# A state-space block with experts on one core: ScalarE's second decay takes over two of VectorE's waits, C rows in four buffers, tanh written into the activation tile

## What is computed

```python
# attention part: INNER = 512 channels d, 16 states n, T = 512 positions t
dt = softplus(xb @ W_dt + b_dt); A = -exp(A_log); B = xb @ W_B; C = xb @ W_C
def step(h, inp):                              # scanned over t
    x_t, dt_t, B_t, C_t = inp
    h = exp(dt_t[:, :, None] * A) * h + (dt_t * x_t)[:, :, None] * B_t[:, None, :]
    return h, einsum('bdn,bn->bd', h, C_t)
y = (y + D_param * xb) * silu(z);  x = x + ga * (h_in + y @ W_out)
# expert part: every expert is computed for every token and weighted (0 for those not picked)
act = silu(x @ gate_e) * (x @ up_e);  out = sum_e weight_e * (act @ down_e)
```

## Time and profile before

| what | value |
|---|---|
| median of 3 runs | 2757.75 us (2750.83 to 2760.53) |
| the profiled execution, its own time | 2752.47 us |
| its span in the trace | 2750.4 us |
| PE, DVE, POOL, ACT busy (share of the span) | 86%, 87%, 81%, 53% |
| DMA engines, mean rate | 217 GB/s |
| granted TensorE clock, mean | 0.942 |

### The profile page before, as it was taken

One profiled execution on the slowest core, in us unless ns is written; L12 is line 12 of the kernel. 1 busy time (PEld: TensorE's weight loads), 2 busy tenths in 40 slices (PEclk: granted clock), 3 DMA queues, 4 the chain that ended last, 5 costly groups with the idle time before them and its releaser, 6 DMA issues.

```text
span 2750.4 us, 28746 instructions
## 1 busy us (share of the span) xinstructions
PE 2365.5 (86%) x9004; PEld 1687.1 (61%) x9004; DVE 2391.1 (87%) x2386; ACT 1455.0 (53%) x2767; POOL 2234.6 (81%) x1563
## 2 busy tenths in 40 slices
PE   3445798999989899998989999898999989898899
PEld 1212566666756666675666667566666656666678
DVE  2679899989999999999999999989999999999922
ACT  3455556555555655555565555556555555654311
POOL 1678888888988888898988888888888889887922
PEclk7677899999999999999999999999999999999999
DMA  4789899999989899998989999898999989898921
GB/s 114 197 197 252 206 244 223 233 236 221 248 212 247 219 245 233 222 246 210 241 219 248 221 213 249 211 235 219 243 228 218 245 206 244 220 248 214 241 59 50
DMA packets 338378, 596.79 MB, mean 217 GB/s; under 512 B 49696, under 2 KB 160288, under 8 KB 338224
## 3 DMA queue, kind: packets, MB, share of 16 engines
q0 software_dynamic: 72960, 243.30, 46.3%
q1 hardware_dynamic: 265264, 351.64, 41.2%
HBM read 349.89 MB, written 10.06 MB: 131 GB/s over the span
## 4 chain that ended last, share of the span: by engine, by line
PE 51%; POOL 15%; DVE 9%; DMA 8%; issue 8%; ACT 7%; SPq 0%; POOLq 0%; DVEq 0%; ACTq 0%
PE wbank L498 16%; PE mbank L510 9%; PE wbank L400 8%; POOL unit L1183 6%; DMA gsum<-unit 6%; DVE hbank L717 5%; PE wbank L440 4%; PE wbank L526 3%; PE wbank L388 3%; POOL act L1150 2%; POOL gsum L1195 2%; PE wbank L411 2%; ACT z L839 2%; PE wbank L523 2%; POOL rstd L1085 2%
## 5 line engine op out<-in xcount | busy, mean ns | idle before, releaser
L1183 POOL TENSOR_TENSOR unit<-dtx,b_bc 128x1024 f32<-128x1024 f32 x512 | 1353.2, 2653 | 4.6 <-DMA gsum<-unit 2.3
L717 DVE TENSOR_TENSOR_SCAN hbank<-hbank,unit 128x1024 f32<-128x1024 f32 x512 | 1173.0, 2291 | 94.7 <-ACT hbank L1012 73.8
L1012 ACT ACTIVATE hbank<-dt,a_neg 128x512 f32<-128x512 f32 x1024 | 667.8, 680 | 266.3 <-DVE unit L731 232.6
L510 PE MATMUL mbank<-down_t,act 128*128 128x256 f32 x2048 | 524.2, 393 | 70.5 <-POOL act L1150 49.9
L731 DVE TENSOR_TENSOR unit<-hbank,c_bc 128x1024 f32<-128x1024 f32 x448 | 546.1, 1219 | 25.6 <-DMA c_bc<-bc_scratch 1.7
L1195 POOL DMA_DIRECT2D gsum<-unit x448 | 448.9, 1002 | 111.3 <-DMA gsum<-unit 59.0
L1150 POOL TENSOR_TENSOR act<-act,w_all 128x512 f32<-128x512 f32 x256 | 362.6, 1417 | 217.3 <-DVE act L695 202.0
L498 PE MATMUL wbank<-h_t,up_t 128*128 128x256 f32 x2048 | 502.3, 389 | 10.4 <-DVE gz L599 10.4
L510 PEld LDWEIGHTS mbank<-down_t,act 128*128 128x128 f32 x2048 | 395.1, 196 | 176.8 <-POOL act L1150 70.5
L498 PE MATMUL wbank<-h_t,gate_t 128*128 128x256 f32 x2048 | 487.2, 381 | 0.0
L498 PEld LDWEIGHTS wbank<-h_t,up_t 128*128 128x128 f32 x2048 | 396.5, 196 | 108.0 <-DVE gz L599 28.8
(11 more groups left out here) (116 smaller groups left out, 2230.6 us busy)
## 6 DMA issues: line engine op xcount, KB each, us to landing
gsum<-unit POOLq DMA_DIRECT2D x448, 512.0 KB, 7.4
c_bc<-bc_scratch SPq DMA_DIRECT2D x464, 256.0 KB, 5.6
b_bc<-bc_scratch SPq DMA_DIRECT2D x448, 256.0 KB, 6.1
w_all<-w_scratch SPq DMA_DIRECT2D x256, 256.0 KB, 4.7
ht<-in_L_attn_x_dram SPq DMA_DIRECT2D x16, 512.0 KB, 5.2
w_out<-in_L_attn_W_out_dram SPq DMA_DIRECT2D x16, 512.0 KB, 6.1
ht<-in_L_attn_x_dram POOLq DMA_DIRECT2D x16, 512.0 KB, 8.6
out_dram<-xt SPq DMA_DIRECT2D x16, 512.0 KB, 3.3
```

Of the source, the lines that this page charges most:

```text
L510: m = eng.matmul(mbank[:, u * H:(u + 1) * H], act[:, (n - 1) % MOE_RING, j, u * P:(u + 1) * P], down_t[:, e, :], start=(e == 0 and u == 0) ...
L717: eng.tensor_tensor_scan(h, h, unit[:, g % RING, :, :].rearrange("p a t -> p (a t)"), 0.0, ALU.mult, ALU.add).then_inc(scanned, 1)
L1012: eng.activation(hbank[g % HB][:, a, :], dt[:, 2 * q + a, :], ACT.Exp, scale=a_neg[:, 2 * q + a, n:n + 1]).then_inc(decayed, 1)
L1183: eng.tensor_tensor(unit[:, g % RING, :, :], dtx[:, 2 * q:2 * q + 2, :], b_bc[:, s:s + 1, :].to_broadcast([P, 2, T]), ALU.mult).then_inc(d ...
```

## The change

Three things are changed. First, the second half of each decay on ACT also waits for `driven` of its unit and for the unit's row of C; the scan on DVE then waits for `decayed` alone and the product for `scanned` alone, since `decayed` now implies the other two. Second, C has four buffers and is loaded three units ahead, as the row is now needed earlier. Third, the tanh of an expert pair is written into the `act` tile itself, and the DVE product works in place; the tanh waits for the down matmuls that last read this buffer, and no longer for DVE's use of the tanh before it.

```diff
-    B_RING, C_RING, W_RING = 4, 3, 2
-    B_LEAD, C_LEAD = 3, 2
+    B_RING, C_RING, W_RING = 4, 4, 2
+    B_LEAD, C_LEAD = 3, 3
...
-        etanh = sb("etanh", [P, 2 * HT])
...
                         need.wait_ge(etanhed, n + 1)
-                        eng.scalar_tensor_tensor(out=a, in0=etanh[:, :], scalar=1.0, in1=t.bank[:, :], op0=ALU.add,
+                        eng.scalar_tensor_tensor(out=a, in0=a, scalar=1.0, in1=t.bank[:, :], op0=ALU.add,
                                                  op1=ALU.mult).then_inc(t.free, 1)
...
             def scan(g):
 
-                need.wait_ge(driven, g + 1)
                 need.wait_ge(decayed, 2 * g + 2)
...
             def times_c(g):
 
-                s, loads, _, _ = c_rows[g]
-                need.wait_ge(c_in[s], 16 * loads)
+                s = c_rows[g][0]
                 need.wait_ge(scanned, g + 1)
...
             def experts(row):
                 for s in range(E + 1):
                     if s < E:
-                        t = work.at["gates2", row, s]
+                        n, t = E * row + s, work.at["gates2", row, s]
                         need.wait_ge(t.full, t.after)
-                        if E * row + s:
-                            used = work.at["gates2", *divmod(E * row + s - 1, E)]
-                            need.wait_ge(used.free, used.after)
-                        eng.activation(etanh[:, :], t.bank[:, :], ACT.Tanh, scale=0.5).then_inc(etanhed, 1)
+                        if n >= MOE_RING:
+                            need.wait_ge(down_done, n - MOE_RING + 1)
+                        eng.activation(act[:, n % MOE_RING, :, :].rearrange("p j t -> p (j t)"), t.bank[:, :], ACT.Tanh,
+                                       scale=0.5).then_inc(etanhed, 1)
...
                 if g >= HB:
                     need.wait_ge(c_scaled, g - HB + 1)
+                s, loads, _, _ = c_rows[g]
+                if a:
+                    need.wait_ge(driven, g + 1)
+                    need.wait_ge(c_in[s], 16 * loads)
                 eng.activation(hbank[g % HB][:, a, :], dt[:, 2 * q + a, :], ACT.Exp,
```

## The result

| what | before | changed |
|---|---|---|
| median (20 runs each) | 2755.02 us (2747.80 to 2761.24) | 2768.09 us (2757.78 to 2782.58) |
| the profiled execution, its own time | 2752.47 us | 2759.93 us |
| its span | 2750.4 us | 2758.2 us |
| mean granted clock | 0.942 | 0.942 |

The ratio is 1.0047, with a 95% interval of 1.0034 to 1.0060: the changed kernel is slower by 13 us. I had forecast 2757 us and no change.

A forecast was written before the change was run, and what follows sets the result against it. No engine was clearly the bound: PE, DVE and POOL were all nearly full, and PE's matmuls led the chain. -1.6 + 0.75 = -0.9 us gave 2751.6 for the profiled execution, 2757 us against the median; range 2743 to 2768.

The forecast's parts named there:

- C, the tanh and the DMAs: C loads, tanh buffer and DMA traffic: C is there in time, 16 fewer loads, tanh never waited for etanh; 0.
- The sum's -1.6 us: Second waits that DVE loses at product and scan, counting only those on the chain: 14 x 0.07 + 10 x 0.06.
- My bound by the chain: Scans on DVE: all 58 scans on the chain get both gains, 58 x 0.13, at most -7.5 us.
- the 14 + 10 pieces on the chain: DVE's extra wait instructions listed on the chain: 14 between scan and product, 10 behind a decay; -1.6 us.
- The first scan, +0.75 us: At the very start the scan waits for POOL's drive, then also the decay and hand-over: it begins 0.75 us later.
- The waits that ACT gains: ACT's second decay waiting for drive and C: late scans and tanhs taken at 0, at worst 3.8 + 5.6 us.
- DVE is the bound: Rival: every gap cut from DVE's queue shortens the run, all 22 us, to 2736; 0.22 for gaining over 8.3 us.
- ACT's queue is held: Rival: decay waiting for POOL holds the tanh, then DVE; 2773 us, or 2788 in full; 0.14 for losing over 8.3 us.
- The change doesn't save the gap: Rival: C's row itself sets the 0.07 us, so scan to product stays 2.39 us; 2758.5 us, chance 0.06.
- DVE's waits for ACT: Sign on DVE: they would stay near 74 us for the scan and 92 us for the tanh.
- If the tanh's row grew by 10 us or more, the second rival has it: Sign: DVE's wait for the tanh growing by 10 us or more would show that ACT's queue is held.
- if the DMA's adds ... changed their time to landing: Sign: the DMA adds onto gsum, held by the chain, changing their landing time would make the forecast wrong altogether.

The follow-up runs named there:

- experiment 3: Kernel before with the tanh written into act, no etanh, four C buffers and a C lead of 3, all waits as before: 2775.58 us, ratio 1.0089.
- experiment 7: experiment 3 with C loaded from the row of the state one unit back, 30 or 34 KB from its B: 2746.58 us, ratio 0.9990.
- experiment 8: Kernel before with only C's row changed, to that of one unit ahead, 32 KB from the B loaded with it: 2789.55 us, ratio 1.0120.
- experiment 4: experiment 3 with the wait for C moved from product to second decay; the scan still waits for the drive: 2766.37 us, ratio 1.0059.
- experiment 10: C's rows stored turned by one state, 34 KB from their B: in the changed kernel 2753.79 us, 0.9987; in experiment 4's kernel 2752.54 us, 0.9979.
- experiments 2: Kernel before with only the tanh written into act, no etanh, and DVE working in place: 2754.00 us, ratio 1.0005.
- experiment 5: Kernel before with the tanh written into act, no etanh, and four C buffers, but the C lead of 2 kept: 2751.80 us, ratio 1.0011.
- the changed kernel turned: Changed kernel with C's rows in DRAM turned by one state, 34 KB from the B of the same state: 2753.79 us, ratio 0.9987.
- experiment 1: Kernel before with only the wait for driven moved from the scan to ACT's second decay: 2751.98 us, ratio 1.0000.

## Why the prediction was wrong, point by point

- **"C, the tanh and the DMAs"** is the part that failed, and there the sentence "448 loads and not 464 ... under 1% of the traffic; 0". I costed a moved load by its count, its bytes and the moment of its release, and count and bytes are as I said. I never asked what it is read beside. The load "now serves the unit after", and the load of B next to it in SP's queue serves that same unit, so their rows fell on 32 KB apart. In place of 0 this term is +0.84% in experiment 3, 22 us by the medians. Moving the address alone takes it away (experiment 7, 0.9990) and brings it into the kernel before (experiment 8, 1.0120). That the rows fall 32 KB apart can be had from the kernel's text: two leads, two row numbers. What it costs can't; only the runs tell that. The trace shows addresses nowhere, and a listing of the order on SP shows the same two loads in the same order.
- **The sum's -1.6 us** had the right sign and was too small. The products start 2.33 us behind their scans wherever they stand directly behind them, and experiments 3 and 4 put the moved wait for C at 9 us of gain; without the clash it is 0.2 to 0.3% (experiment 10's 0.9979 and 0.9987, against 1.0005 and 1.0011 for experiments 2 and 5), 5 to 9 us, though for the changed kernel turned the intervals touch. That all of it comes from the 253 shorter gaps is argued, as no run takes them away by themselves. My bound by the chain, 7.5 us, was nearly right; the 14 + 10 pieces on the chain were too few. I take it that the chain of one execution names one path where others are almost as long, so that a gap off it is still worth something. The Trainium skill ("VectorE: DVE Perf Modes", The DRAIN you can't avoid), which has a semaphore cost a chain on VectorE nothing, would have made this 0. For a second wait the rows disagree: 2.39 us from scan to product with it, 2.33 without.
- **The first scan, +0.75 us.** It starts at 91.26 and not 90.25. POOL's first drive itself starts 0.30 us later (88.17 and not 87.87), so the decay behind the drive costs 0.71 us. Right; in experiment 1 and in the changed kernel turned, too, the scan starts 3.10 us after the drive, and in the kernels whose scan keeps the wait 2.38 to 2.40.
- **"The waits that ACT gains": 0 for the late tanhs and late scans.** Right by experiment 1, at 1.0000 with 291.7 us of ACT's waiting. With the rows turned, moving the drive's wait as well changes 0.9979 to 0.9987, nothing that can be told. The idle time only changed its name, as I had said, but for the larger part it was not the waits for PE that gave way: the decays' own wait for DVE fell by 130.6 us.
- **The rivals.** "DVE is the bound" (2736 us) is false: the gap went from all 253 products, and the moved wait for C brought 5 to 9 us, where this rival has 17.7 for it and 22 with the scans. "ACT's queue is held" (2773 us) had the right sign and almost the right size, for a cause that isn't there: experiment 1 has its mechanism and none of its loss. "The change doesn't save the gap" is false by the timeline.
- **The signs I named.** The EVENT_SEMAPHOREs fell by 976 on DVE and ACT's wait for POOL appeared, as said. DVE's waits for ACT didn't stay near 74 and 92 us; they are 103.7 and 115.8. "If the tanh's row grew by 10 us or more, the second rival has it": it grew by 23.3 us, and the rival has not got it. In experiment 4, where the decay never waits for the drive, the row is 112.0 us at a loss of 0.6%; in experiment 8, where the address alone is another, it grows from 92.5 to 106.8. A wait row that both theories can lengthen tells neither. The other sign, "if the DMA's adds ... changed their time to landing", was nearer: the adds' landing moved only from 7.4 to 7.5 us, but POOL's wait for them went from 59.0 to 75.9.
- **The range** ended at 2768 and the median is 2768.09. Its upper end came from a third of the false rival's price, so that it nearly holds is luck. Its width had no room for a transfer term, which I had given no ends: a term set at 0 from both sides because its bytes don't change.

## What to carry to other kernels

When a prefetch distance changes, write down which addresses are then read at the same time: a lead moved by one cost 0.8% here by pairing DRAM rows 32 KB apart, where count, bytes and waits had no part in it. Test such a suspicion by moving the address alone, in both directions (experiments 7 and 8), since landing medians moved by just 0.3 to 0.4 us and the waits rose at transfers that have nothing to do with it. Take the parts of a change one by one before believing the one whose wait row grew most: the conspicuous 314 us of ACT waiting cost nothing that could be told, and what looked like bookkeeping of buffers was the loss.

## What the runs showed of the hardware that I had not expected

- Two loads that read 2 KB rows of DRAM, each spread over 128 partitions and both in flight, can disturb each other by the distance of their rows. Counted from C to the B issued ahead of it, 32 KB and a mix of 24 and 40 (with some 8 and 56) KB cost time, and 26 and 38, 28 and 36, 30 and 34 KB don't. Counted from C to the B issued behind it, 24 and 40 KB cost nothing that could be told. In the kernel before, 32 KB costs 1.20% [1.01, 1.38]. Across all kernels the medians to landing are 6.3 to 6.6 us for B and 5.7 to 5.9 for C with the clash, and 6.1 to 6.3 and 5.4 to 5.7 without (experiment 5's C, 6.6 us, aside). What in the memory clashes was not tried and stays open; so does whether 16 KB, or 8 KB by itself, does it, and why the changed kernel, at 1.0047 against 0.9987 with its rows turned, loses 0.6% where the kernel before loses 1.2%. Two things that bear on the last: with the rows turned half of the loads of C still have a B behind them at 32 KB, and the kernel of experiment 8 alone has the 20.3 us more of waiting for the experts' weights.
- A second wait costs an instruction on DVE 0.06 to 0.07 us when it stands right behind the one it waits for (scan to product, 2.39 against 2.33 us). On ACT, where the second decay has it behind the first, it costs nothing that can be told (0.9987 [0.9974, 1.0001] with it, 0.9979 [0.9968, 0.9990] without, in the kernels with turned rows).
